# Moving the second norm's transposes, the router, the value projection and one transposed maximum to other slots of an attention body

## The reference

```python
mod = (silu(c) @ wmod)                        # shifts, scales and gates of each batch
h = layernorm(x) * (1 + ca) + sa
x = x + ga * attention(h)                     # 16 heads of 8 channels, softmax over 512 keys
h = layernorm(x) * (1 + cb) + sb
scores = softmax(h @ w_router)                # 8 experts, the best two weighed
x = x + gb * sum_e comb[e] * ((silu(h @ w_gate[e]) * (h @ w_up[e])) @ w_down[e])
```

## Time and profile before

| | us |
|---|---|
| median of 3 timed runs | 670.53 |
| lowest and highest | 670.4, 673.66 |
| profiled execution, its own time | 679.32 |
| its span, first to last instruction | 677.5 |
| mean granted TensorE clock of the span | 0.954 |

### The profile page before, as it was taken

How to read it: one execution, slowest core, us unless ns; L and a number is a source line. 1 busy time by engine, 2 the same in 40 slices (tenths; PEclk the granted TensorE clock), 3 DMA queues, 4 the chain that set the end, 5 groups by cost and what they waited for, 6 DMA issues and landing times.

```text
span 677.5 us, 12806 instructions
## 1 busy us (share of the span) xinstructions
PE 618.2 (91%) x3349; PEld 282.1 (42%) x3349; DVE 546.4 (81%) x1033; ACT 442.1 (65%) x843; POOL 267.2 (39%) x384
## 2 busy tenths in 40 slices
PE   4199999999999999999999999899889999999996
PEld 3112223323332323332322332124667777777774
DVE  3588898989988989988988989414888888888885
ACT  1206778878868878868878878756654555555553
POOL 4521012222222222222222212423567776776763
PEclk9757999999999999999999999858999999999999
DMA  6712604304304304304304301154234444445401
GB/s 177 165 69 53 213 4 95 129 19 96 128 20 95 127 17 95 127 18 95 127 17 95 127 17 47 46 155 108 93 117 135 141 142 140 133 132 151 137 36 31
DMA packets 49084, 65.58 MB, mean 97 GB/s; under 512 B 9544, under 2 KB 30544, under 8 KB 49040
## 3 DMA queue, kind: packets, MB, share of 16 engines
q1 hardware_dynamic: 46416, 64.32, 32.5%
q10 hardware_dynamic: 2624, 0.79, 0.5%
HBM read 47.26 MB, written 17.83 MB: 96 GB/s over the span
## 4 chain that ended last, share of the span: by engine, by line
PE 41%; issue 17%; POOL 16%; DVE 15%; ACT 6%; DMA 2%; SPq 1%; POOLq 1%; DVEq 0%; ACTq 0%
PE o_acc L1169 14%; POOL hid_lo L601 13%; PE s_row L1142 11%; DVE negmax L853 10%; PE s_col L1155 7%; ACT probs L645 3%; DVE probs L1032 2%; PE misc L1107 1%; SPq L308 1%; POOL h_lo L607 1%; PE misc L1093 1%; PE misc L1090 1%; PE misc L1123 1%; DMA k_stack<-k_scr 1%; DVE bn L829 1%
## 5 line engine op out<-in xcount | busy, mean ns | idle before, releaser
L853 DVE TENSOR_REDUCE negmax<-s_row 128x1 f32<-128x512 f32 x512 | 321.7, 681 | 45.4 <-PE s_row L1142 39.9
L645 ACT ACTIVATE probs<-s_col 128x512 f32<-128x512 f32 x512 | 271.9, 599 | 82.0 <-PE s_col L1155 79.9
L1142 PE MATMUL s_row<-k_stack,q_stack 64*128 64x512 bf16 x512 | 146.6, 402 | 27.4 <-DMA k_stack<-k_scr 13.9
L601 POOL TENSOR_TENSOR hid_lo<-probs,hid_hi 128x512 fp32r<-128x512 f32 x87 | 128.5, 1494 | 62.7 <-ACT hid_hi L789 62.7
L1155 PE MATMUL s_col<-q_stack,k_stack 64*128 64x512 bf16 x512 | 137.8, 391 | 5.5 <-ACT probs L645 4.9
L1169 PE MATMUL o_acc<-probs,v_aug 128*32 128x512 f32 x1024 | 141.8, 627 | 0.0
L1142 PEld LDWEIGHTS s_row<-k_stack,q_stack 64*128 64x128 bf16 x512 | 36.6, 93 | 189.1 <-DVE negmax L853 142.5
L789 ACT ACTIVATE hid_hi<-probs 128x512 fp32r<-128x512 f32 x88 | 55.6, 632 | 86.4 <-DVE probs L1032 86.3
L1032 DVE TENSOR_TENSOR probs<-probs,q_stack 128x512 f32<-128x512 f32 x56 | 62.3, 1113 | 15.7 <-POOL hid_lo L601 13.5
L509 POOL CAST negmax_parts<-negmax 128x16 bf16<-128x16 f32 x32 | 6.3, 197 | 157.8 <-DVE negmax L853 157.8
L1022 DVE TENSOR_TENSOR probs<-probs,s_col 128x512 f32<-128x512 f32 x88 | 59.5, 676 | 2.2 <-ACT probs L809 2.1
(11 more groups left out here) (134 smaller groups left out, 683.8 us busy)
## 6 DMA issues: line engine op xcount, KB each, us to landing
q_scr<-q_parts SPq DMA_DIRECT2D x48, 128.0 KB, 2.4
k_scr<-k_parts SPq DMA_DIRECT2D x48, 128.0 KB, 2.4
q_stack<-q_scr SPq DMA_DIRECT2D x8, 768.0 KB, 6.8
k_stack<-k_scr SPq DMA_DIRECT2D x8, 768.0 KB, 8.0
q_stack<-combT_scr SPq DMA_DIRECT2D x24, 256.0 KB, 3.3
k_stack<-combT_scr SPq DMA_DIRECT2D x16, 224.0 KB, 2.8
q_stack<-combT_scr SPq DMA_DIRECT2D x16, 192.0 KB, 2.7
q_stack<-combT_scr SPq DMA_DIRECT2D x16, 160.0 KB, 2.6
```

What stands on the lines that cost most here:

```text
L601: nc.gpsimd.tensor_tensor(hid_lo[k % HIDDEN][:], weighed[(par + k) % 2], hid_hi[k % HIDDEN][:], ALU.subtract).then_inc(s["hid_split"], 1)
L645: nc.scalar.activation(probs[t % 2][:, j, :], s_col[score_bank("col", u)][:], ACT.Exp, scale=INV_SCALE).then_inc(s["exp_done"], 1)
L853: nc.vector.tensor_reduce(negmax[n % 2][:, j, qc:qc + 1], s_row[score_bank("row", u)][:], AX.X, ALU.max, negate=True).then_inc(s["row_max" ...
L1142: nc.tensor.matmul(s_row[score_bank("row", u)][:], q_stack[par][at:at + KS, head // 2, P * qc:P * (qc + 1)], k_stack[par][at:at + KS, head ...
```

## The change

`x1T` goes from (10, 2) to (10, 0), `router` from (11, 1) to (11, 0), `v` from (9, 0) to (8, 0), and `max3` from (8, 1) to (8, 2). The five steps of the second norm's statistics, which stood at five places from (6, 1) to (8, 1), are done at three, the last at (7, 1). No instruction is added or removed.

```diff
     TASKS = {
         (0, 0): "xT", (0, 2): "max1", (1, 0): "q", (2, 0): "k", (3, 0): "o0", (4, 0): "o1", (4, 2): "max2",
-        (5, 0): "attnT", (6, 0): "proj", (8, 1): "max3", (9, 0): "v", (10, 2): "x1T", (11, 1): "router",
+        (5, 0): "attnT", (6, 0): "proj", (8, 0): "v", (8, 2): "max3", (10, 0): "x1T", (11, 0): "router",
         (12, 1): "max0", (15, 0): "combT",
     }
...
-            LN2_STATS = [(6, 1), (7, 0), (7, 1), (8, 0), (8, 1)]
+            LN2_STATS = {(6, 1): (0, 1), (7, 0): (2, 3), (7, 1): (4,)}
...
-                            if at in LN2_STATS:
-                                ln2_stats(b - 1, LN2_STATS.index(at))
+                            for step in LN2_STATS.get(at, ()):
+                                ln2_stats(b - 1, step)
```

## The result

The changed kernel takes 664.45 us in the median of four runs (662.96 to 666.58), the kernel before 672.1 in four (670.4 to 676.13): a ratio of 0.985, 95% interval 0.981 to 0.989. Measured again beside other kernels, six runs gave 663.91 against 675.42 in eleven of before, a ratio of 0.986 (0.981 to 0.992). The forecast was 662.9, in a range of 658.5 to 670.0. Five of the 29 executions of before that stand beside f1 to f4 were over 1.5% above its fastest; the medians and ratios there leave them out. A ratio comes with the interval beside it and need not be the quotient of the two medians to the last digit.

A forecast was written before the change was run, and what follows sets the result against it. No engine is full; the handover loop between TensorE and VectorE, 2.70 us a slot, was taken as the bound. Gains of 6.2 (six middle bodies), 1.4 (last) and 0 (first) took 670.53 to 662.9 us, range 658.5 to 670.0.

The forecast's parts named there:

- Slots 10 and 11: Middle body: with `x1T` and `router` filling TensorE's wait, both slots together take 5.85 us for 7.16, gain 1.31.
- Slots 7 to 9: Middle body: bunched statistics and more load on ScalarE lose 0.28 us, bounds nothing to 0.88.
- a full ScalarE: Three slots, 8.7 us: ScalarE full to nine tenths, so slot 9's first exponential comes a little late for the fourth column product.
- strict order: ScalarE's first in, first out queue: by that rule alone each of three moved copies would cost its wait, 0.76 us.
- The norm's chain: GpSimd's chain from statistics to `x1n`: with earlier statistics it ends at 285.29, a margin of 0.45 us before `x1T`.
- One body: One middle body gains 1.03 us (1.31 − 0.28), ends 0.31 and 1.40; six give 6.2.
- `max0`: At (12, 1), needing slot 11's split of the maxima: just in time, costing 0 to 0.1 us.
- The last body: Last body gains 1.4 us (0 to 2.6): 1.0 from `max3`'s wait, 0.4 from `x1T` and `router`, `x1n` being late.
- The clock: Timed runs mostly kept full clock, the profiled execution being 8.8 us over the median; the change moves them by its sum alone.
- the sum: Whole kernel: 6.2 from six middle bodies, 1.4 from the last, 0 from the first, 7.6 us in all.
- half clock before, full after: Rival: timed runs had half clock too, and the shorter wait at `max3` now keeps full clock: 654.1 us, chance 0.08.

The follow-up runs named there:

- f1: Kernel before, with ScalarE's rounding of the last body's second expert weight moved from (6, 1) to (6, 0): 671.64 us, ratio 0.998 to before.
- f4: Changed kernel with outputs saved behind the first exponential of slots 1 and 9, and second expert weight rounded at (6, 0): 668.94 us, ratio 0.994 to before.
- e1: Kernel before with only `x1T` and `router` moved, to (10, 0) and (11, 0): 670.01 us, ratio 0.995 to before.
- e4: Kernel before with only `router` moved, to (11, 0): 674.50 us, ratio 1.000 to before.
- e3: Kernel before with `v`, `max3` and the statistics moved as in the change, `x1T` and `router` left: 674.49 us, ratio 1.000 to before.
- f3: Changed kernel with ScalarE's saving of the outputs put behind the first exponential of slots 1 and 9: 670.41 us, ratio 0.994 to before.
- g3: Changed kernel with only the store of the transposed maxima moved, to (1, 1) and (9, 1): 663.71 us, ratio 0.983 to before.
- g0: The changed kernel unaltered, run again for comparison on one chip: 663.91 us, ratio 0.986 to before.
- e2: Kernel before with `x1T`, `router` and the statistics moved, `v` and `max3` left at (9, 0) and (8, 1): 666.54 us, ratio 0.987 to before.
- g1: Changed kernel with outputs saved behind the first exponential of slots 1 and 9, and the maxima's store at (1, 1) and (9, 1): 663.95 us, ratio 0.985 to before.
- f2: Changed kernel with the last body's second expert weight rounded at (6, 0), not (6, 1): 661.19 us, ratio 0.982 to before.
- g2: Changed kernel with later output saving, maxima's store at (1, 1) and (9, 1), and second expert weight rounded at (6, 0): 665.48 us, ratio 0.987 to before.

## Why the prediction was right, and where it was not

**Slots 10 and 11.** Taken 5.85, measured 5.86 (2.71 and 3.15). That a task in the middle of a slot costs only what goes beyond TensorE's wait for VectorE held here. e1 and e4 break one dependence each, and what their slots are longer by is a wait that the trace shows right ahead of the task (1.28 and 0.47); e4's was found only after its forecast of 3.65 had missed.

**Slots 7 to 9.** Taken 0.28 as a loss, measured 0.30, alone (e3) and with the rest. Slot 7 costs 0.19 by the bunched statistics. Slot 8 costs 0.17 and slot 9 gives back 0.06. Two reasons were partly wrong. `v` did not cost slot 8 what it cost slot 9; it hides behind VectorE's delay. And slot 9's late exponential was put down to a full ScalarE; f3 and g3 show the issue of the store in it. ScalarE was fuller than said, too: 6.2 us of exponentials, 0.60, 0.60 and 0.78 of copies and 0.27 for `max3`'s make 8.4 of 8.7 us, not nine tenths. That its copies would cost their waits in full, as the prediction priced one reading of its strict order, did not come: in the changed kernel it idles 0.17 ahead of `max3`'s copy and shows no idle time ahead of `v`'s or `h2T`'s.

```profile
275.90 0.60 ACT L684 ACTIVATE v_aug<-misc 128x512 f32<-128x512 f32 x1
...
282.13 0.78 ACT L699 ACTIVATE h2T<-misc,mod 128x512 f32<-128x512 f32 x1
```

**The norm's chain.** `x1n` was forecast 0.45 us ahead of `x1T`, it is 0.57 ahead. e1 shows what lies behind that margin: 1.28 us a body.

**One body.** 1.03 forecast, measured 1.01 by slots and 1.03 by windows (50.30 − 49.27). Six of them are 6.1 us.

**`max0`** comes 0.31 after the last column product, as anywhere: no wait, in the bounds of 0 to 0.1.

**The last body.** A wait of some 1.2 us at `x1T` was forecast. It is 0.93. Of `max3`'s wait about 0.2 is left. The 1.4 us that the last body was to give cannot be read from these two profiles, the clocks being different. For the 0.4 of `x1T` and `router` there is a pair: e3 and g0 kept the full clock through the last body, in 48.05 and 47.56 us, 0.5 apart. The 1.0 for `max3` has no such pair and is not shown; e2, where `max3` stays, has a last body of 48.29 us with 6.8 at half, the changed kernel 49.66 with as much, which does not bear it out.

**The clock: the step that failed.** The prediction took it that the timed runs mostly kept the full clock, since the profiled execution was 8.8 us over their median. They did not. Of 63 later timed runs of the kernel before, the mean granted clock is between 0.948 and 0.973, and the medians of their three groups are 674.42 to 675.42, so 670.53 was a low sample of three. The profiled execution, at 0.954, is one of a spread.

What the clock costs can be read from these 63 runs, on three chips. Time at half clock in a run is 2 × (1 − clock) × span, on average 52.8 us, of which 34.1 lie ahead of body 1 in the profiled execution. A straight line through half-clock time and time has a slope of 0.34 us per us and leaves a standard deviation of 0.9 us; the last bodies of the changed kernel and g0, the same program, agree with it (49.66 − 47.56 = 2.1 us for 6.8 at half). The ten runs of the changed kernel (four of the result, six of g0) have 45.0 us at half clock on average and a mean time of 664.80, where the 63 have 674.30. Of these 9.5 us, 7.9 × 0.34 = 2.7 go with the clock, and 6.8 are left at equal clock: 6.1 for the bodies and 0.7 for all else, where the sum had 1.4. So the terms that were worked out are about right, 6.8 for 7.6, and there is a term that the sum left at nothing, the clock's 2.7. The 7.9 has a standard error of about 1.9, so this term is less certain than the 6.8.

The same line turns the timed runs of the experiments into a test of the slots. Mean time against the mean of before, in us; the last column is six times the difference of the sums of slots 7 to 11 in the table above, with slot 1 where it differs:

| kernel | as timed | at equal clock | six bodies by slots |
|---|---|---|---|
| changed | −9.5 | −6.8 | −6.1 |
| e1 | −4.4 | −1.7 | −0.7 |
| e2 | −8.7 | −6.4 | −5.5 |
| e3 | +0.6 | +2.1 | +1.8 |
| e4 | −0.7 | −2.2 | −1.6 |
| f3 | −4.0 | −1.3 | −1.1 |
| g1 | −10.1 | −6.6 | −6.6 |
| g3 | −10.3 | −8.3 | −8.0 |

At equal clock every kernel lies within 1.0 us of what its slots say; as timed, up to 3.7 away. e3 and e4, both "no change" by their ratios, are slower and faster by what the slots say. f2, at −7.3, is only 0.5 below the changed kernel, so most of its lead is clock; the 1.5 of its last body is not told from this within the scatter.

The rival "half clock before, full after" is right in its condition, that the timed runs had the half clock too, and wrong in its size: the changed kernel falls as well, and 2.7 came of its 8.8. Why the changed kernel spends less time at half is open. That the shorter waits of the last body do it is not shown: e1, which keeps the wait at `max3`, has the same 45 us at half as the changed kernel, and g2, with the shorter waits, has 51.

That the time came within 1.6 us of 662.9 is thus owed in part to luck, two errors of opposite sign: a base that was 3.8 us low (674.3 for 670.53) and a gain that was 1.9 short (7.6 for 9.5).

## What to carry to other kernels

Where two engines hand a few banks back and forth, first find the wait in the loop, and then put other work of the engine at the point where it would wait, not beside its longest uninterruptible piece. Then follow what the moved step reads: here the place was worth 1.3 us a body only with the statistics earlier (e1) and with a full slot between two dependent tasks (e4). Do not set a profiled execution against a median of three to infer a clock; look at the granted clock of each run, and compare kernels at equal time at half clock: here that turned three timed results that seemed to contradict the slots (e1, e3, e4) into ones that agree with them within 1.0 us.

## What was not expected of the hardware

- A transfer issued from ScalarE takes 0.32 us of ScalarE's own order, and with the wait for the copy that it stores 0.54 us stood bare (f3). With one other instruction of 0.58 handed over before it, most of this vanished; moving a copy that seemed to be in the way made two slots of each body 0.2 to 0.5 us longer.
- The granted clock fell after 3.40 us with 1.78 busy, and in another execution of the last body, with a wait of 0.94 at `x1T` (g0), it did not; once at half it stayed there for 27.3 us although TensorE was busy 25.59 of them. The Trainium skill (TensorE: Matmul & The Clock Gate, Why this matters for your kernels) names idle gaps between bursts of matrix products as what to avoid. These traces agree, and show that short gaps can be enough: in the last bodies no gap of TensorE ahead of a fall was over 1.38 us (f1).
